# Attention of a macaron block: the first iteration starts after 46 of 144 row-maximum pieces, and its first eight steps carry the other 98

## The reference

```
q = (x @ wq.T) -> 16 heads of 16;  k, v = (x @ wk.T), (x @ wv.T) -> 4 heads of 16, each used by 4 heads of q
attn = einsum('bqhd,bkhd->bhqk', q, k) / sqrt(16);  causal mask;  softmax over k
out  = einsum('bhqk,bkhd->bqhd', attn, v) @ wo.T
```

## Time and profile before

| | |
|---|---|
| median of 3 runs | 8606.55 us (8600.69 to 8619.03) |
| the profiled execution, its own time | 8600.78 us |
| span of its trace, first to last instruction | 8599.0 us |
| PE busy, share of the span | 7649.1 us, 89% |
| DVE busy | 7351.8 us, 85% |
| ACT busy | 5097.1 us, 59% |
| mean granted TensorE clock | 0.951 |
| first pieces of the two attentions reduced from | 207.14 us and 6463.10 us |

### The profile page before, as it was taken

The page is one execution under the profiler, slowest core; times in us unless marked ns, Lnnn a source line. Parts: engine busy times, 40 slices in busy tenths (PEclk is TensorE's granted clock), DMA queues, the critical chain, the costliest instruction groups (busy, mean ns, idle before and its releaser), DMA issues. The chain is left out here.

```text
span 8599.0 us, 133275 instructions
## 1 busy us (share of the span) xinstructions
PE 7649.1 (89%) x38899; PEld 3079.3 (36%) x38900; DVE 7351.8 (85%) x10758; ACT 5097.1 (59%) x7698; POOL 3712.1 (43%) x1828
## 2 busy tenths in 40 slices
PE   6999999989898888888888888888779999999899
PEld 3333333335543333333333333333443333333355
DVE  6988888958868999999979999999458988988588
ACT  3577777762256666666656555555224777777622
POOL 0010111000018999999969999999300010011000
PEclk8899999989999999999999999999987999999899
DMA  6101111012262222222233333333561011011122
GB/s 174 17 20 19 19 21 25 13 45 75 67 234 85 83 82 83 83 83 82 82 100 101 101 99 101 101 97 100 166 196 29 20 19 20 19 19 19 37 72 65
DMA packets 542812, 617.68 MB, mean 72 GB/s; under 512 B 195969, under 2 KB 353921, under 8 KB 538081
## 3 DMA queue, kind: packets, MB, share of 16 engines
q1 hardware_dynamic: 537568, 576.35, 22.8%
q0 software_dynamic: 4608, 33.56, 1.9%
HBM read 411.41 MB, written 163.76 MB: 67 GB/s over the span
## 5 line engine op out<-in xcount | busy, mean ns | idle before, releaser
L833 DVE TENSOR_REDUCE ffn_att_mx<-psum 128x1 f32<-128x512 f32 (+3 forms) x4608 | 2725.7, 653 | 354.9 <-PE psum L674 199.4
L794 ACT ACTIVATE ffn_att_e<-psum,unscale 128x1024 f32<-128x1024 f32 (+3 forms) x2560 | 2378.7, 985 | 750.0 <-PE psum L739 744.0
L641 POOL TENSOR_SCALAR_AFFINE_SELECT ffn_att_e<-ffn_att_e 128x512 f32<-128x512 f32 x512 | 326.1, 637 | 3007.8 <-ACT ffn_att_e L794 3007.8
L674 PE MATMUL psum<-ffn_att_k,ffn_att_q 48*128 48x512 f16 (+3 forms) x5120 | 1433.5, 366 | 173.5 <-DMA ffn_att_v<-v 58.1
L1697 POOL TENSOR_TENSOR scan_r_h<-scan_r_h,scan_r_cs 128x1024 f32<-128x1024 f32 x512 | 1207.7, 2451 | 148.2 <-ACT scan_r_state L1860 144.7
L1697 POOL TENSOR_TENSOR scan_f_h<-scan_f_h,scan_f_cs 128x1024 f32<-128x1024 f32 x512 | 1204.7, 2446 | 117.0 <-ACT scan_f_state L1860 114.8
L705 PE MATMUL psum<-ffn_att_e,ffn_att_v 128*32 128x512 f32 (+3 forms) x10240 | 1234.2, 555 | 8.0 <-ACT ffn_att_o L809 2.6
L1776 PE MATMUL psum<-scan_f_h,ident 128*128 128x512 f32 x2048 | 1002.5, 630 | 83.9 <-POOL scan_f_h L1697 83.4
L1776 PE MATMUL psum<-scan_r_h,ident 128*128 128x512 f32 x2048 | 980.6, 620 | 75.3 <-POOL scan_r_h L1697 74.5
L1900 ACT ACTIVATE psum<-scan_r_dt,scan_r_an 128x512 f32<-128x512 f32 x1024 | 698.0, 682 | 460.2 <-DVE scan_r_h L1992 460.0
L674 PEld LDWEIGHTS psum<-ffn_att_k,ffn_att_q 48*128 48x128 f16 x5120 | 394.5, 94 | 1554.0 <-DVE ffn_att_mx L833 1268.3
(11 more groups left out here) (261 smaller groups left out, 9895.2 us busy)
## 6 DMA issues: line engine op xcount, KB each, us to landing
scan_f_cs<-scan_f_bcd SPq DMA_DIRECT2D x264, 256.0 KB, 3.1
scan_r_cs<-scan_r_bcd SPq DMA_DIRECT2D x264, 256.0 KB, 3.2
scan_f_bs<-scan_f_bcd SPq DMA_DIRECT2D x82, 256.0 KB, 3.4
scan_r_bs<-scan_r_bcd SPq DMA_DIRECT2D x82, 256.0 KB, 3.4
scan_f_win<-xp SPq DMA_DIRECT2D x18, 1036.0 KB, 6.7
scan_r_win<-xp SPq DMA_DIRECT2D x18, 1036.0 KB, 7.0
mamba_out_ys<-yz SPq DMA_DIRECT2D x18, 1024.0 KB, 7.3
scan_r_yi<-y SPq DMA_DIRECT2D x17, 1024.0 KB, 9.3
```

The costliest lines, as they stand in the source:

```text
L674: ins = nc.tensor.matmul(psum[:, turn, j * w:(j + 1) * w], q[at, i // HALF, pair, i % HALF * P:(i % HALF + 1) * P], k[at, c * P:c * P + w] ...
L794: nc.scalar.activation(E[:, s % PB, 2 * hp:2 * hp + 2, off:CH], psum[:, 2 * hp:2 * hp + 2, off:CH], ACT.Exp, scale=unscale[:, 0:1]).then_i ...
L833: nc.vector.reduce_max(mx[:, hh * 2 + pairs[0]:hh * 2 + pairs[1], i // HALF, i % HALF, c // TT], psum[:, turn, 0:(pairs[1] - pairs[0]) * w ...
```

## The change

The prelude ends after T0 = NP0 + 6 = 46 pieces. In the iteration called "first" (iteration 0), the tail that steps 0 to 7 share out is pieces 46 to 143 and no longer 116 to 143. All other iterations, and steps 8 to 39 of the first one, have the shares they had. `share` now takes the name of the iteration's kind, and the wait of line 656 is on T0 reductions.

```
--- before.py
+++ after.py
@@ -492,19 +492,24 @@
     assert NP0 + 4 < T < NP
     head = spread(list(range(T)), steps[D:], beside)
     tail = spread(list(range(T, NP)), steps[:D], beside)
+    T0 = NP0 + 6
+    assert T0 < T
+    first_tail = spread(list(range(T0, NP)), steps[:D], beside)
...
-    def share(s, last=False):
-
-        return [("tail", n) for n in tail[s]] if s < D else [] if last else [("head", n) for n in head[s - D]]
+    def share(s, when):
+
+        if s < D:
+            return [("tail", n) for n in (first_tail if when == "first" else tail)[s]]
+        return [] if when == "last" else [("head", n) for n in head[s - D]]
...
                     if found is None:
-                        pe.wait_ge(m_red, T)
+                        pe.wait_ge(m_red, T0)
                         return
...
                 pe.wait_ge(loaded[0], LOADS)
-                for n in range(T):
+                for n in range(T0):
                     if n >= 3:
                         pe.wait_ge(m_red, n - 2)
                     maximum(0, n, 5 + n % 3)
...
                 dve.wait_ge(recip, 1)
-                for n in range(T):
+                for n in range(T0):
                     reduce(0, n, 5 + n % 3)
```

More of the change, by code:

```diff
@@ L506, in attention @@
         for s in range(NB):
-            uses += share(s, when == "last")
+            uses += share(s, when)
             qb = back_close(s)
@@ L743, in score @@
                                 ins.then_inc(s_ps, 1)
-                        todo = share(s, when == "last")
+                        todo = share(s, when)
                         half = len(todo) // 4 * 2
@@ L870, in step @@
                             split_low(it + 1, 0, turn_bank(when, ("max", 0)))
-                        for kind, n in share(s, when == "last"):
+                        for kind, n in share(s, when):
                             reduce(it if kind == "tail" else it + 1, n, turn_bank(when, (kind, n)))
```

## The result

The changed kernel takes 8623.04 us in the median of 22 runs (8607.60 to 8635.68), the kernel before 8606.72 us (8600.21 to 8619.03, 22 runs). The ratio is 1.0017, with a 95% interval from 1.0010 to 1.0023: 9 to 20 us slower. The forecast was 8610.9 us, and its sum had +4 us; the medians differ by 16.3 us. The range and the direction held, the size didn't.

What follows compares the result with a forecast made beforehand. DVE alone was taken to bound the prelude, with gaps waiting for PE in the first steps. Per attention, 3.3 us wait, less 5.1 or 5.2 gaps, plus 4.0 small gaps: +4.3 us overall, 8610.9 us, range 8595 to 8624.

Steps and rivals of the forecast that it cites:

- DVE's total is fixed, and bounds the gain: Up to `negate` at step 7's end, DVE has the same reductions in either order, 58.1 us; gain at most 10.3 us.
- the stretch from piece 45 to the negate of g = 1: Sign: from piece 45's end to `negate` at step 7's end, 61 to 67 us against 63.2; shorter than 61 meant wrong.
- The gaps of before go: DVE's three gaps before the first shared pieces and in steps 2 and 6 vanish: 5.1 and 5.2 us per attention.
- The wait for the maxima: After piece 45, step 0's scores wait for line 588's DMAs; DVE idles 3.3 us, bounds 3.1 to 5.8.
- Small gaps behind `weighted`: In steps 2 to 7, PE's other work outlasts DVE's three buffered pieces: 0 to 5.7 us per attention, by clock.
- the method: Gap sum in the steps: PE's time from last piece to DVE's restart, less 1.74 us of buffered pieces; checked on 1.55 us.
- I take the lower clock for seven tenths of the gaps: 4.0 us per attention: In the first eight steps, mostly single pieces were to keep the clock low, costing 4.0 us of the 5.7 per attention.
- the 0.2 us for scores alone in three steps: Within the first eight steps, scores without `weighted` were to leave DVE a 0.2 us gap in each of three steps.
- Rival B: Low clock outlasts the eight steps, making PE the bound from step 8: +27 us, 8633 us; chance 0.08.
- Rival A: Clock rises to 1.00 within the first steps and stays, so small gaps vanish: -3.7 us, 8602.9 us; chance 0.18.
- rival C: Maxima's DMAs before step 0 land after 3.7 us, not 1.7; each attention loses 2.0 us more: 8614.9 us; chance 0.05.
- rival D: ACT's 41.5 us of waiting in the prelude, or part of it, is gained, over 17 us; chance 0.03.

Runs made afterwards that it cites:

- bunching: Against the changed kernel, no piece stands between scores and `weighted` in steps 0 to 7 of iteration 0, the whole share following `weighted`; 106.3 and 105.5 us by DVE's measure.

## Why the prediction was right, and where its size was off

*DVE's total is fixed, and bounds the gain.* Right. Without its gaps the stretch from piece 45 to the negate of g = 1 is 68.7 - 10.06 = 58.6 us; 58.1 was worked out. That ACT's first exponential came 37 us earlier brought nothing.

*The gaps of before go.* Right: 5.1 and 5.2 us of them, the drain now inside the longer wait.

*The wait for the maxima.* Right, 3.27 and 3.25 us against 3.3. TensorE stood idle in it for 3.1 us and not 1.7, at the low clock both before and behind it. The run with 52 pieces shows it by taking it away.

*Small gaps behind `weighted`.* The mechanism is shown by bunching (larger gaps), by 80 pieces (nearly the same gaps) and by the clock at 1.00 (gaps of 0.3 us). PE's timeline has the pattern of the method; in step 6 of the changed kernel `weighted` and the next pieces are

```profile
281.42 1.93 PE L710 MATMUL psum<-ffn_att_e,ffn_att_v 128*32 128x512 f32 x8
283.29 1.03 PE L679 MATMUL psum<-ffn_att_k,ffn_att_q 48*128 48x512 f16 x3
```

with DVE's restart at 283.93 and a gap of 1.30, where 1.2 was worked out.

**The step whose size was off** is "I take the lower clock for seven tenths of the gaps: 4.0 us per attention". The clock was at 0.50 for practically the whole stretch (0.53 over it in the second attention), and the gaps came to 6.8 us, 2.8 us per attention more than the 4.0. Taking seven tenths was 1.7 us of this. The other 1.1 us are terms of the sum, which even in full gave only 5.7. The gap at the 384-column `weighted` of step 3 was 1.31 and not 0.7 us; the pieces next to it are on the diagonal, and DVE's release there is a mask matmul (L683). The transposes of step 6 left 0.45 + 0.67 us and not 0.6. The `weighted` of the other steps cost 0.1 or 0.15 us more than worked out, and the 0.2 us for scores alone in three steps did not appear.

*Rival B in small.* The low clock outlasted the eight steps, but by 1.5 and 3 us and not by eight steps. From the negate of g = 1 to the next one took 28.8 and 29.5 us where before took 27.7 and 27.7: 1.2 and 1.8 us more. The forecast had nothing for it. With both corrections its sum is +4.3 + 5.6 + 3.0 = +12.9 us; the trace shows 13.6 and the medians 16.3. Rival A (clock rises early), rival C (late landing) and rival D (a large gain) did not happen.

*What was luck.* The measured +16.3 us is nearly four times the sum's +4.3. It is also beyond the largest sum of the forecast, +13 us or 8619 us; only the 5 us added to that for scatter hold it inside the range. Of the signs that the prediction gave, the stretch from piece 45 to the negate of g = 1 (68.7 us) lies outside its 61 to 67 us. And a difference below 0.2% could be told after all: with 22 runs of each kernel the interval of the ratio excludes 1.

## What to carry to other kernels

Where one engine works without a break, an earlier start of the others brings at most that engine's own gaps; count these first. Then count what covers the start: here six more pieces hide all but 0.7 us of a 3.3 us wait for small DMAs. And a buffer of three pieces that covers the neighbour's other work at one clock of TensorE may not cover it at the other, so take a stretch's durations from rows at the clock that the new order will have, and don't assume that it is the faster one.

## What the runs showed of the hardware

TensorE's granted clock did not follow its busy time. With half-height matmuls doubled it had matmuls for 56 of 56 us, with full-height ones added for 112 of 112 us, and the clock was 0.50, its 1.2 GHz level, in both. In the second attention of the latter run it rose after 96 us of the same. In the ten traces every rise in the first eight steps and just behind them, but one, came during a `weighted` or shortly behind one: in before at 281.5 us, in the `weighted` of step 3, and in the changed kernel at 302.75 us, in that of step 8. But most `weighted` had no rise behind them, and no run separates what counts there.

A full-height matmul between half-height ones cost more than its columns. With 512 columns each and at the low clock they start 0.54 us apart (240.41, 240.95, 241.49 us in the run with one ahead of each piece), a pair in 1.08 us. The two copies of a half-height matmul in the run with doubled pieces start 0.40 us apart (239.73, 240.13).

The scatter of the later iterations goes with such clock changes, too. Three iterations of the second attention of the changed kernel, with the same instructions in each (the first takes 99.3, the second 102.6, the third 97.7 us):

```profile
6596.20:6695.50 99.30, 94.35 (x790) 31.59 (x786) 88.15 (x156) 76.50 (x87) 10.15 (x16) 0.98 0.13 20
6695.50:6798.10 102.60, 98.07 (x790) 33.30 (x786) 88.29 (x157) 76.57 (x88) 10.14 (x16) 0.93 0.09 20
6798.10:6895.80 97.70, 92.86 (x790) 31.84 (x786) 88.13 (x157) 76.53 (x87) 10.15 (x16) 1.00 0.11 21
```

The iteration in which the clock dropped for some 14 us (mean 0.93) took 4.9 us more than the one in which it never did. In seven of the ten traces, such iterations took 97.7 to 97.9 us at a mean clock of 1.00, 98.8 to 99.5 us at 0.98 and 102.5 or 102.6 us at 0.93. The fifth, eighth and eleventh of an attention took longer in all seven, 102.5 to 110.8 us, at 0.89 to 0.97. Whether the clock or a stall comes first there isn't shown.
